# Two-layer graph network on one core: eight consecutive nodes per partition, and a last chunk that ends as three tiles and one

## The reference

```python
# layer 0
sim     = tanh(adj * adj)                        # simlar is adj
new_adj = top-350 of each row of sim * (adj > 0) # all entries, when a row has at most 350
h2      = tanh(x @ W_proj + b_proj)
x1      = layernorm(x + relu(new_adj @ (h2 @ W_gcn) + b_gcn))
# layer 1
pos = (adj > 0) @ x1;  neg = (adj < 0) @ x1
out = layernorm(x1 + concat(pos, neg) @ node_w + node_b * diag(adj)[:, None]
                   + (adj @ x1) @ edge_w + edge_b * diag(adj)[:, None])
```

## Time and profile before

| | |
|---|---|
| median of 3 runs | 609.61 us (609.23 to 611.47) |
| profiled execution, its own time | 610.62 us |
| its span, first to last instruction | 608.8 us |
| PE busy | 600.5 us (99%) |
| DVE, ACT, POOL busy | 471.2 (77%), 420.4 (69%), 187.7 (31%) |
| DMA | 130.67 MB, mean 215 GB/s |
| chain that ended last | PE 92%, DMA 5%, DVE, POOL and ACT 1% each |

### The profile page before, as it was taken

One profiled execution on the slowest core, in us unless ns is written; L12 is line 12 of the kernel. 1 busy time (PEld: TensorE's weight loads), 2 busy tenths in 40 slices (PEclk: granted clock), 3 DMA queues, 4 the chain that ended last, 5 costly groups with the idle time before them and its releaser, 6 DMA issues.

```text
span 608.8 us, 5805 instructions
## 1 busy us (share of the span) xinstructions
PE 600.5 (99%) x1972; PEld 342.3 (56%) x1972; DVE 471.2 (77%) x690; ACT 420.4 (69%) x315; POOL 187.7 (31%) x88
## 2 busy tenths in 40 slices
PE   9999999999999999999999999999999999999996
PEld 6644444444444444555655656655665665657995
DVE  3767978888797979986497697697697697697843
ACT  3687686868768686558874865965865875865960
POOL 0598798887979697000000000000000000000000
PEclk9999999999999999999999999999999999999999
DMA  8999999999999991049787586586595685775000
GB/s 231 339 340 348 333 332 312 314 280 316 273 340 265 344 208 1 11 128 259 215 240 199 164 249 194 167 234 199 140 270 159 173 240 155 216 197 157 2 17 20
DMA packets 139455, 130.67 MB, mean 215 GB/s; under 512 B 9763, under 2 KB 139430, under 8 KB 139430
## 3 DMA queue, kind: packets, MB, share of 16 engines
q1 hardware_dynamic: 74390, 66.22, 39.3%
q10 hardware_dynamic: 65040, 64.17, 36.7%
HBM read 128.27 MB, written 2.10 MB: 214 GB/s over the span
## 4 chain that ended last, share of the span: by engine, by line
PE 92%; DMA 5%; DVE 1%; POOL 1%; ACT 1%; SPq 0%; issue 0%; DVEq 0%; ACTq 0%
PE acc L1059 34%; PE acc L1045 32%; PE stage L1068 10%; PE stage L1067 10%; DMA a_rows<-in_adj_dram 4%; PE stage L1059 2%; PE to_rows L1074 1%; PE to_rows L1073 1%; PE stage L1007 1%; PE to_rows L1024 1%; DMA x_rows<-in_x_dram 0%; POOL a_cols L390 0%; DVE a_cols L662 0%; ACT a_cols L593 0%; PE stage L1002 0%; POOL a_cols L384 0%
## 5 line engine op out<-in xcount | busy, mean ns | idle before, releaser
L662 DVE STREAM_TRANSPOSE a_cols<-a_rows 128x2048 f32<-128x2048 f32 x120 | 277.2, 2317 | 92.9 <-PE stage L1068 63.4
L1045 PE MATMUL acc<-a_cols,rhs 128*128 128x512 f32 x512 | 221.8, 593 | 1.8 <-ACT a_cols L593 1.1
L1059 PE MATMUL acc<-a_cols,x_rows 128*128 128x512 f32 (+1 forms) x512 | 212.3, 565 | 0.0
L1045 PEld LDWEIGHTS acc<-a_cols,rhs 128*128 128x128 f32 x512 | 96.4, 190 | 121.5 <-issue 117.8
L390 POOL TENSOR_TENSOR a_cols<-a_cols 128x1536 f32<-128x1536 f32 x56 | 153.2, 2747 | 35.0 <-DVE a_cols L662 34.6
L1059 PEld LDWEIGHTS acc<-a_cols,x_rows 128*128 128x128 f32 x512 | 96.6, 190 | 96.3 <-issue 92.4
L611 ACT ACTIVATE a_rows<-a_rows 128x4096 f32<-128x4096 f32 x32 | 116.1, 3627 | 46.2 <-DVE a_cols L662 38.1
L593 ACT ACTIVATE a_cols<-a_cols 128x2048 f32<-128x2048 f32 x56 | 107.1, 1912 | 49.8 <-POOL a_cols L390 49.2
L614 ACT ACTIVATE a_rows<-a_rows 128x4096 f32<-128x4096 f32 x32 | 115.9, 3621 | 1.0
L1067 PE MATMUL stage<-masks,x_hi 128*128 128x512 f32 (+1 forms) x288 | 115.0, 408 | 0.0
L1068 PE MATMUL stage<-masks,x_lo 128*128 128x512 f32 (+1 forms) x288 | 103.0, 366 | 0.0
(11 more groups left out here) (119 smaller groups left out, 271.5 us busy)
## 6 DMA issues: line engine op xcount, KB each, us to landing
a_rows<-in_adj_dram ACTq DMA_DIRECT2D x120, 512.0 KB, 10.4
a_rows<-in_adj_dram SPq DMA_DIRECT2D x120, 512.0 KB, 10.6
out_dram<-n_rows SPq DMA_DIRECT2D x28, 64.0 KB, 7.5
x_rows<-in_x_dram ACTq DMA_DIRECT2D x8, 64.0 KB, 2.5
x_rows<-in_x_dram SPq DMA_DIRECT2D x8, 64.0 KB, 2.4
x_rows<-in_x_dram ACTq DMA_DIRECT2D x4, 128.0 KB, 3.9
x_rows<-in_x_dram SPq DMA_DIRECT2D x4, 128.0 KB, 4.1
diag<-in_adj_dram SPq DMA_DIRECT2D x32, 0.5 KB
```

Source lines behind the costliest of these rows:

```text
L662: nc.vector.transpose(half_out(hs), half_in(s, h % HALVES)).then_inc(turned[layer], 1)
L1045: last = nc.tensor.matmul(acc[parity][:], rhs[:, b, :], a_cols[:, h % HSLOTS, k, :], start=(b == 0), stop=(b == BLOCKS - 1))
L1059: last = nc.tensor.matmul(sums, x_rows[:, b, :], rows(a_cols[:, h % HSLOTS, k, :]), start=(b == 0), stop=(b == BLOCKS - 1))
```

## The change

1. **Eight consecutive nodes on one partition.** Node = span*1024 + partition*8 + block. Chunk c is the rows whose number is c modulo 8, over the whole matrix. The transposes now read `a_rows` with a step of eight elements (32 bytes). x is loaded as contiguous runs of 2 or 4 KB, in two DMAs of 64 partitions per part instead of four of 32, and in five parts instead of six. An output chunk is one DMA of 128 partitions instead of four; the diagonal is four DMAs instead of 32. In the DMAs of `adj` a partition reads 16 runs of 1 KB as before, but rows that neighbouring partitions read are 8 rows (128 KB) apart instead of 2 (32 KB), and the 16 rows of one partition 256 rows (4 MB) apart instead of 64 (1 MB).
2. **The boundary.** Rows finished last in layer 0 are now block 7 of every span, so each odd half has one block that has to wait. `first_chunk` runs halves 0 to 3 without these blocks, waits once, does the two left-out blocks, then halves 4 to 7. DVE does the whole last normalization behind half 3.
3. **The end.** Parts of three tiles and one. Four halves (TOGETHER = HSLOTS) go apart instead of three. The first count matmuls stand ahead of the mask matmuls of part 0 instead of behind them. DVE branches on the flag before it copies part 0's mask sums. For the last tile DVE negates the mean, ACT subtracts it while DVE takes the root, and DVE only multiplies. The last stores are one DMA per queue and part.

```diff
-    PARTS = [(0, TILES // 2), (TILES // 2, TILES // 2)]
-    TOGETHER = 3
+    PARTS = [(0, TILES - 1), (TILES - 1, 1)]
+    TOGETHER = HSLOTS
-    X_PARTS = [4, 4, 4, 4, 8, 8]
+    X_PARTS = [4, 4, 8, 8, 8]
+    QUEUE_HALF = [slice(0, P // 2), slice(P // 2, P)]
...
         def quarter_in(rows, s, q):
-            span, half = rows
-            src = adj[bass.ds(span * SPAN, SPAN), s * SPAN + q * PCOLS:s * SPAN + (q + 1) * PCOLS]
-            return src.rearrange("(r i h) k -> h i r k", h=2, i=SQ)[half]
+            src = adj[:, s * SPAN + q * PCOLS:s * SPAN + (q + 1) * PCOLS]
+            return src.rearrange("(r i b) k -> b i r k", b=PB, i=SQ)[rows]
...
         def x_in(part, k):
             span, at = divmod(x_starts[part], PB)
-            return x_blocks[span][q][:, at // 2:(at + X_PARTS[part]) // 2, :]
+            return x_spans[span][QUEUE_HALF[k], at * F:(at + X_PARTS[part]) * F]
...
         def half_in(slot, h):
-            return a_rows[:, slot, :, :].rearrange("p r (m j e) -> p e r m j", j=SQ, e=2)[:, h]
+            return a_rows[:, slot, :, :].rearrange("p r (j b) -> p r b j", b=PB)[:, :, h * HB:(h + 1) * HB, :]
...
         def part_of(cols, at, tiles):
-            return cols.rearrange("p (q m i) -> p q m i", q=QUARTERS, i=SQ)[:, :, at:at + tiles, :]\
-                .rearrange("p q m i -> p q (m i)")
+            return cols[:, at * P:(at + tiles) * P]
...
             def first_chunk():
-                for h in range(HPC):
-                    if h == 0:
-                        pe.wait_ge(lo_ready, CHUNKS - 1)
-                    if h == HPC - HALVES:
-                        pe.wait_ge(lo_ready, CHUNKS)
+                waiting = [h for h in range(HSLOTS) if h % HALVES]
+                pe.wait_ge(lo_ready, CHUNKS - 1)
+                for h in range(HSLOTS):
                     pe.wait_ge(masked, h + 1)
-                    with_adj(acc[0][:], h, all_rows)
+                    ready = range(HB - 1) if h in waiting else range(HB)
+                    with_adj(acc[0][:], h, all_rows, ready)
...
+                pe.wait_ge(lo_ready, CHUNKS)
+                for h in waiting:
+                    with_adj(acc[0][:], h, all_rows, [HB - 1])
+
+                    with_masks(acc_m[0][:], h, all_rows, [HB - 1]).then_inc(half_used[1], 1 if h == 1 else 2)
+                for h in range(HSLOTS, HPC):
+                    pe.wait_ge(masked, h + 1)
+                    with_adj(acc[0][:], h, all_rows)
+                    with_masks(acc_m[0][:], h, all_rows).then_inc(half_used[1], 1)
...
                     if not before:
-                        if h in (3, 4, 5):
-                            norm0(LAST, h - 3)
+                        if h == HSLOTS - 1:
+                            for part in range(3):
+                                norm0(LAST, part)
...
+            act.wait_ge(mean_negated, 1)
+            for k in range(tiles):
+                ins = nc.scalar.activation(n_rows[:, LAST[2], at + k, :], last_rows[1][k], ACT.Identity,
+                                           bias=minus_mean[:, k:k + 1])
+            ins.then_inc(centred, 1)
...
                 def scaled():
                     waited(ln_step, base + LN_STEPS)
+                    if root_of:
+
+                        at = PARTS[root_of][0]
+                        rows = n_rows[:, LAST[2], at:at + tiles, :]
+                        waited(centred, 1)
+                        nc.vector.tensor_tensor(rows, rows, r.unsqueeze(2).broadcast_to([P, tiles, F]), ALU.mult)\
+                            .then_inc(normed, 1)
+                        return
```

More of the change, by code:

```diff
@@ L312, in rows_of @@
         def rows_of(layer, chunk):
-            return (chunk[1] * -1 + (PIECES - 1), 1 - chunk[2]) if layer else (chunk[1], chunk[2])
+            return CHUNKS - 1 - chunk[0] if layer else chunk[0]
         def next_of(chunk):
-            c, span, parity = chunk
-            return c + 1, span + parity, 1 - parity
+            return chunk[0] + 1, None, 1 - chunk[2]
         def is_first(c):
@@ L398, in _, with load_x @@
         def _(sp):
-            def load_x(g):
-                for q in SP_QUARTERS:
-                    sp.dma_start(x_of(g, q), x_in(g, q)).then_inc(x_loaded[g], 16)
+            def load_x(part):
+                sp.dma_start(x_of(part, 0), x_in(part, 0)).then_inc(x_loaded[part], 16)
             def load_piece(rows, s):
@@ L445, in store @@
                 sp.wait_ge(normed, CHUNKS + c + 1)
-                for q in range(QUARTERS):
-                    sp.dma_start(rows_out(rows, q),
-                                 n_rows[SQ * q:SQ * (q + 1), parity, :, :]).then_inc(stored[parity], 16)
+                sp.dma_start(rows_out(rows), n_rows[:, parity, :, :]).then_inc(stored[parity], 16)
             def layer1(chunk, before):
@@ L630, in _ @@
                 act.wait_ge(last_summed, part + 1)
[L631 to L633 removed]
+                nc.scalar.copy(part_of(z_t, at, tiles), last_acc[part][:, 0:tiles * P]).then_inc(sums_kept, 1)
                 act.wait_ge(ln_step, LN_STEPS * (2 * CHUNKS - 1 + part) + 2)
@@ L1034, in layer0 @@
                     if not before:
-                        for g in range(h // HALVES * HALVES, h // HALVES * HALVES + 2):
-                            emptied(pe, USES.index(("rhs", g)))
+                        emptied(pe, USES.index(("rhs", h)))
                     if before:
@@ L1054, in all_rows, with with_adj @@
                 return cols
-            def with_adj(sums, h, rows):
-                for k in range(HB):
+            def with_adj(sums, h, rows, part=range(HB)):
+                for k in part:
                     b = block_of(h, k)
@@ L1061, in with_adj, with with_masks @@
                 return last
-            def with_masks(sums_m, h, rows):
-                for k in range(HB):
+            def with_masks(sums_m, h, rows, part=range(HB)):
+                for k in part:
                     b = block_of(h, k)
@@ L1178, in last_chunk @@
                 last.then_inc(last_summed, 1)
-                for h in range(apart, HPC):
-                    pe.wait_ge(masked, LAST[0] * HPC + h + 1)
-                    last = part_masks(h, 0)
-                last.then_inc(last_masked, 1)
                 pe.wait_ge(stats_step, 1)
@@ L1187, in last_chunk @@
                 last.then_inc(stats_pe, 1)
+                for h in range(apart, HPC):
+                    pe.wait_ge(masked, LAST[0] * HPC + h + 1)
+                    last = part_masks(h, 0)
+                    if h == apart:
+                        pe.wait_ge(stats_step, 4)
+                        nc.tensor.matmul(stats_at[0:1, CHUNKS:CHUNKS + 2], ones[:, 0:1], fails[:], start=True,
+                                         stop=True).then_inc(stats_pe, 1)
+                last.then_inc(last_masked, 1)
                 part_adj(apart, 1)
                 part_masks(apart, 1)
-                pe.wait_ge(stats_step, 4)
-                nc.tensor.matmul(stats_at[0:1, CHUNKS:CHUNKS + 2], ones[:, 0:1], fails[:], start=True, stop=True)\
-                    .then_inc(stats_pe, 1)
                 pe.wait_ge(y_ready, 2 * CHUNKS - 1)
```

120 lines of the change are left out of this document (53 added, 67 removed).

## The result

| | before | after |
|---|---|---|
| median (runs) | 609.68 us (6, 609.23 to 611.47) | 722.77 us (6, 721.33 to 727.88) |
| ratio | | 1.1865, 95% interval 1.1821 to 1.1909 |
| profiled execution: time, span | 610.62, 608.8 | 727.88, 726.1 |
| PE, DVE, ACT busy | 600.5, 471.2, 420.4 us | 644.2, 673.1, 423.4 us |
| granted clock, mean | 0.998 | 0.957 |

The account below looks back on a forecast made before the run. PE, without idle time in mid-layer, was taken as the bound. Head -1.5, middle and boundary 0, end +0.7 gave -0.8 us on 610.62, so 609.8; 1.0 lower for the median, 608.8 us, range 606.0 to 615.0.

Parts of the forecast that it names:

- The middle: Layers 0 and 1 between head and end: no change in time, 0 us, since PE is full there.
- I cost both at nothing: Mid-layer: the new addresses of the transposes and of the `adj` loads cost 0 us.
- the decision point: Transpose time from which DVE bounds a layer instead of PE: 2.85 us in layer 0, 3.5 in layer 1.
- rival A: Both layers: transposes pay for the 32-byte step and DVE bounds; 4.5 us each if doubled, some 778 us; chance 0.10.
- The head: Start of the kernel: fewer DMAs ahead of `adj`, whose loads start about 3 us earlier; -1.5 us, ends -2.2 and +1.3.
- when enough bytes have landed: Start of the kernel: bytes landed set its end; 3.2 us to win at most, half taken, 1.6.
- +1.3 for a late first part of x: Start of the kernel: PE may start 1.3 us later, x's first part coming in one 128 KB DMA per queue.
- The boundary: Between layers 0 and 1: rows ready at 260.9 us, PE needs them at 268.4; cost 0, bounded at +1.
- The end: Last chunk and tail: +1.5 narrow masks, +0.5 stall, +0.2 row matmuls, -1.5 tail, +0.7 us; ends -1.8 and +4.7.
- B: Layer 0: `adj` loads slow down from rows 128 KB and 4 MB apart; 643 us at 260 GB/s; chance 0.07.
- D: Start and end of the kernel both come out well, -3.8 us, 605.8 us; chance 0.17.
- Freeing DVE earlier is worth nothing in itself: Last chunk: DVE's earlier branch wins no time, as part 0's work was already hidden; it makes room for the third tile.

Follow-up runs that it names:

- before_pitch: Kernel before, with its `adj` loads reading the rows that the changed kernel reads (every eighth row of the matrix): 610.39 us, ratio 0.9996.
- steps: Separate kernel of single instructions at several read and write steps, no DMA beside them: DVE transpose 2312 ns at 8 bytes, 3790 at 16, 3835 at 32.
- before_step3: Kernel before, with its transposes reading `a_rows` at a step of three elements (12 bytes) instead of two: 625.93 us, ratio 1.0253.
- after_step2: Changed kernel, with its transposes reading `a_rows` at the old step of two elements instead of eight: 614.98 us, ratio 1.0061.
- before_newend: Kernel before, with the change's whole new end except that its last stores stay two DMAs per queue and part: 613.2 us, ratio 1.0046.
- after_xparts: Changed kernel with transposes at the old step of two elements and x loaded in six parts instead of five: 614.58 us, ratio 1.0079.
- after_xquarters: `after_xparts` with each part of x in four DMAs of 32 partitions instead of two of 64: 613.64 us, ratio 1.0059.
- before_means: Kernel before, with only DVE's branch ahead of the copy of part 0's mask sums and ACT subtracting the last part's mean: 616.55 us, ratio 1.0105.

## Why the prediction was wrong, by its steps

**The failed step** is in "The middle": "I cost both at nothing", of the transposes and the loads of `adj`. For the loads of `adj` that was right (`before_pitch`). For the transposes it was wrong by some 108 of the 113 us. A transpose took 3.93 us instead of 2.32, past the 2.85 from which DVE bounds layer 0. The prediction had what it took to see it: a trace whose reads all had steps of 8 bytes or less, and the decision point. It took the absence of a cost at 8 bytes as evidence against one at 32, though `steps` shows that a step of 8 bytes is free and one of 16 is not, so that the earlier trace rows told nothing between the two. The rule of the Trainium skill that it cites under rival A, "Advanced Engine Details and Errata", section "Memory Cachelines", also lets a step of 8 bytes go free and not one of 32.

**Rival A** had the mechanism and the order of events right, and its size too high: 3.93 us a transpose for its 4.5, layer-0 chunks of 35.9 us for 41.3. In layer 1 its model, 8 x 3.9 + 16.8 = 48.0, comes near the 48.7 measured, but by DVE's time alone; the trace shows DVE and PE handing a pause to each other, with PE at its lower clock behind each pause, which the model did not have.

**The decision point**, 2.85 us, agrees with 2.9 from the trace of after and with the 2.8 to 2.9 of `before_step3`; no run places it more closely.

**The head**, forecast at -1.5: it lost instead. The kernels' times give +1.6 by the medians (`after_step2`, 4.4 above before, against `before_newend`, 2.8 above it) and +0.9 by the ratios. The first matmul with `adj` is 1.2 us later in `after_xparts` than in `after_xquarters`, and 2.8 later in the changed kernel than before; such places scatter between executions (`before_newend`, whose head is before's, begins layer 1 1.1 us later). Two steps failed. The seven DMAs took 0.67 us each to issue and not 0.43, so the loads of `adj` started at 5.46 us, 1.85 earlier and not 3. And the head does not end "when enough bytes have landed": PE's chain on x was as long. The prediction kept its +1.3 for a late first part of x, but PE began on the first part only 0.2 us late; it began on the second at 7.42 us instead of 5.52. DMA in the first 14 us moved 218 GB/s in `after_xparts` and 221 in after, not above 260.

**The boundary**, 0: right. In `after_step2`, whose layer 1 begins 3.8 us later than before, POOL's split ends at 264.83 (forecast 260.9 + 3.8 = 264.7), and PE goes on without a wait at 272.25 (forecast 268.4 + 3.8 = 272.2):

```profile
263.54 1.29 POOL L365 TENSOR_TENSOR x_lo<-x_rows,x_hi 128x512 fp32r<-128x512 f32 x1 [15.83 <-ACT x_hi L551]
```

```profile
272.25 1.02 PE L1052 MATMUL acc<-a_cols,x_rows 128*128 128x512 f32 x2
```

**The end**, +0.7: measured +2.8. The mis-sized term is the narrow mask matmuls. No run shows the prediction's 0.084 us for one; they stood 0.112 apart: +3.3 for +1.5. The trace of before pointed higher: there a load of 32 weight columns took 112 ns (PEld, L1185) and one of 128 columns 189 (L1068), so 96 more columns cost 0.077 us. On top of the 0.044 us between two matmuls of L1185 (0.35/8) an estimate from these rows is 0.12. The two forms of `adj` matmuls add 0.6 (0.329 + 0.112 against 2 x 0.216), forecast 0. The stall was 0.18 for 0.5. The tail won 0.6 (after) to 0.85 us (`before_newend`, by the start of the last mask matmul) for 1.5. Of that, the 0.4 for one store per queue did not come: `before_newend` keeps two and has the shorter tail, its last stores landing in 1.4 to 1.6 us, the single ones of `after_step2` in 1.9 to 2.2. With the 0.2 for row matmuls this adds up to 3.4 us; the interval of the ratio is 2.0 to 3.6.

**The range.** The prediction says that 606.0 to 615.0 leaves out A and B and little else. It also leaves out D's own 605.8.

**"Freeing DVE earlier is worth nothing in itself"** is not contradicted in the changed kernel, where no run has the late branch beside it. In the old order of the end it is a loss of 6 us.

## What to carry to other kernels

Before a layout is changed, list the byte step of every engine read and write that it touches, and ask of each whether the trace has a row with a step as large; steps up to 8 bytes say nothing about 12, 16 or more. If it has none, the trace is no evidence, and a small kernel of single instructions settles it. Compute for each engine the duration at which it takes over, and where an uncovered cost could pass that point, do not give that case a chance as small as that of an accident. An edit that moves a branch or a copy is judged by who is queued behind it in the final order, since the same edit can be free or cost 6 us.

## What the runs showed of the hardware

- Float32 with a step of up to 8 bytes in SBUF is free on DVE; 12 bytes costs 1.25 times (reading; writing was not run), 16 bytes or more 1.62 to 1.68 times, the same for reading and for writing. ACT, reading: 1.07 times at 8 bytes, 2.0 from 16.
- A mask matmul (fp32r) with 128 x 128 weights takes 0.112 us for 128 columns, 0.12 for 256, 0.18 for 384 and 0.23 for 512: narrowing below 256 saves nearly nothing.
- Pauses of PE were followed by several microseconds at the 1.2 GHz level: in after, a granted clock of 0.51 for 5.9 us behind the 3.10 us at 463.68, and 0.50 for 5.9 us behind the 4.86 at the counts; in `before_means`, 0.72 over 6 us behind 3.86. That pause and the slow stretch together cost the kernel 6.1 us.
- From the last small operation on the flag to the next instruction behind the branch DVE needs 3.8 to 4.0 us (3.83 in before, 3.97 in `before_means`).
